# Sorted experts: weights copied to a fixed place by GpSimd, running counts on VectorE, and the last norms further behind

## The chip, the cores and the metric

The kernel runs on one core of one Trainium2 chip. The metric is the device time in microseconds of one execution, the median of several. "us" below is always microseconds, and times inside an execution count from the first instruction of the profiled one.

## The reference

Two transformer layers over x of 4 x 512 rows of 256 numbers, all in float32. Layer 0 is an attention with a delta-rule recurrence and a feed-forward block, layer 1 an attention with one key head. The last block, which the change concerns, is a mixture of eight experts. Each row picks one expert:

```python
def _L1_ffn_ref(x, Wg, W, b):
    logits = jnp.einsum('bsh,he->bse', x, Wg)
    probs = jax.nn.softmax(logits, axis=-1)
    idx = jnp.argmax(probs, axis=-1)
    onehot = jax.nn.one_hot(idx, E, dtype=x.dtype)
    combine = onehot * probs
    y = jnp.einsum('bsh,ehd->bsed', x, W) + b
    out = jnp.einsum('bsed,bse->bsd', y, combine)
    return out
...
x = _layernorm(x + _L1_ffn_ref(x, L1_ffn_Wg, L1_ffn_W, L1_ffn_b), axis=-1)
```

with E = 8 experts, W of 8 x 256 x 256 and b of 8 x 256.

## The kernel before, in words

The kernel is one program with its queues and semaphores written out by hand. Each phase is a block in which every engine has a list of instructions that it works off in order; a `wait_ge` holds all that stands behind it in the same list. The phases are the projections and the delta rule of layer 0, its attention, its feed-forward, the attention of layer 1 with its output projection (`phase_out_proj`, which also loads the experts' weights `We` and biases `be`), and `phase_moe`.

`phase_moe` sorts the 2048 rows by expert, so that a tile of 128 sorted rows needs the weights of one expert alone. Every expert's rows start at a new tile, so there are at most NTS = 16 + 7 = 23 tiles, and 23 are always worked off.

First VectorE derives from the logits a 0/1 choice `oh` for each of NT = 16 tiles of rows and 8 experts. The slot of a row is the number of rows of its expert ahead of it, plus the first slot of the expert. The rows ahead come from TensorE: a product with a triangle for the row's own tile, and 15 products with `ones` for the tiles before (L2099), each recorded as two passes. The count of each expert comes from `cs`, the sum of `oh` over the tiles (L2191), and one more product (L2102). VectorE then works out slots and the expert of each sorted tile (L2197 to L2210), GpSimd scatters the rows to `sorted_d` in DRAM with 16 indirect DMAs (L2165), and SyncE and ScalarE load them back as sorted tiles `xs`.

Then comes the loop over the 23 tiles t:

- TensorE transposes tile t+1 (`sortedT`, L2113), reads the expert's number of tile t into a register (`value_load`, L2117), multiplies with `We[:, k, e, :]` for k = 0, 1 (L2122) and adds the bias by a product of height 1 (L2123). A float32 product appears in the trace as two passes.
- ScalarE copies the transposed rows out of PSUM (L2144), then takes the root for the norm of tile t-1 (`ln.std`, L881) and writes the normalized rows of tile t-3 (`ln.apply_act`, L897).
- VectorE waits for the product of tile t, adds the residual (L2217), and does the small steps of the norm: `rstd` (L885) of tile t-1, statistics of tile t (L871), `shift` (L891) of tile t-1, mean and variance of tile t (L875). `apply_act` waits for `shift`.
- GpSimd waits for the normalized rows of tile t (`y_ok`) and scatters them to the output by an indirect DMA (L2170).

The names in the trace: `moe_sorted_rows` is xs, `moe_sorted_T` is xT, `moe_out_rows` is yo, `moe_tile_expert` the experts' numbers. Engine queues with a q behind the name (PEldq, POOLq) are the sequencer's own instructions.

## Time and profile before

| | us |
|---|---|
| median of 3 runs | 1114.26 |
| lowest, highest | 1113.63, 1125.29 |
| the profiled execution's own time | 1116.42 |
| its span, first to last instruction | 1114.7 |
| TensorE products busy | 948.9 (85%) |
| VectorE busy | 601.9 (54%) |
| ScalarE busy | 459.4 (41%) |
| GpSimd busy | 287.8 (26%) |
| mean granted clock of TensorE | 0.791 of 2.4 GHz |

The rows shown further below come from this one execution. Shares of busy time are means over all phases; what an edit in the last phase is worth has to be read from that phase, which takes from about 985 us to the end.

### The profile page before, as it was taken

Reading aid. Unit: us, or ns where it says so; the run is one execution under the profiler, and the core shown is the slowest. Engines: PE = TensorE matmul, PEld = TensorE weight load, DVE = VectorE, ACT = ScalarE, POOL = GpSimd, SP = SyncE. Lnnn points to the kernel's source line nnn. Section 1 sums busy time; section 2 is a strip of 40 time slices with the busy share of each in tenths; the row PEclk is TensorE's granted clock in tenths of the full one; section 3 lists DMA queues with packets and bytes.
Section 4 is the critical chain, followed back from the end, with each engine's and each line's share of the span. In section 5 each row is a group of like instructions: output and inputs, shape, how many; then the busy total and the mean of one; then the engine's idle time right before and its main releaser. Section 6 shows DMA issues by size and latency. Waiting matters only on the chain. (4 is left out here: it accounts for less than half of the span.)

```text
span 1114.7 us, 21534 instructions
## 1 busy us (share of the span) xinstructions
PE 948.9 (85%) x7997; PEld 617.9 (55%) x7997; DVE 601.9 (54%) x2027; ACT 459.4 (41%) x1046; POOL 287.8 (26%) x538
## 2 busy tenths in 40 slices
PE   6866715899789999979998899898999998952996
PEld 3545715777645555559874455444555554851553
DVE  1874793565467777634435344504777772820332
ACT  2553502000026666642237764631566664620232
POOL 1761112455503333310003000000333333214222
PEclk9985558555569999998879998597999999955555
DMA  5145533422200720020000000000000000405000
GB/s 116 30 84 121 192 100 104 90 61 64 57 2 1 211 58 1 1 86 1 1 21 5 1 1 1 1 1 1 2 2 1 2 1 21 171 15 169 28 30 22
DMA packets 51458, 52.28 MB, mean 47 GB/s; under 512 B 8771, under 2 KB 42905, under 8 KB 51098
## 3 DMA queue, kind: packets, MB, share of 16 engines
q1 hardware_dynamic: 41514, 39.59, 13.1%
q10 hardware_dynamic: 7488, 5.53, 2.0%
q0 software_dynamic: 2352, 5.79, 1.5%
q8 instruction: 64, 1.05, 0.4%
q14 instruction: 40, 0.32, 0.1%
HBM read 26.73 MB, written 20.88 MB: 43 GB/s over the span
## 5 line engine op out<-in xcount | busy, mean ns | idle before, releaser
L816 DVE CUSTOM_DVE_ANT_0 l_masked_scores<-psum,mask_q_rows 128x384 bf16<-128x384 f32 (+3 forms) x512 | 225.0, 488 | 76.1 <-PE psum L763 75.1
L838 ACT ACTIVATE l_probs<-psum 128x512 f32<-128x512 f32 (+1 forms) x384 | 186.3, 527 | 149.7 <-PE psum L749 149.1
L851 POOL TENSOR_SCALAR_AFFINE_SELECT l_probs<-l_probs 128x256 f32<-128x256 f32 x256 | 101.0, 406 | 379.7 <-ACT l_probs L838 379.5
L763 PE MATMUL psum<-kb_heads,q_heads 32*128 32x384 f32 (+3 forms) x512 | 108.4, 505 | 10.7 <-DVE l_neg_max_rows L805 8.7
L763 PE MATMUL psum<-l_k_heads,l_q_heads 32*128 32x384 f32 (+3 forms) x512 | 109.4, 509 | 4.6 <-DVE l_neg_max_rows L805 2.7
L749 PE MATMUL psum<-l_q_and_max,l_k_heads 32*128 32x256 f32 (+3 forms) x512 | 112.3, 472 | 0.0
L749 PE MATMUL psum<-l_q_and_max,kb_heads 32*128 32x256 f32 (+3 forms) x512 | 111.1, 467 | 0.0
L781 PE MATMUL psum<-l_probs,rows_32k 128*32 128x512 f32 (+3 forms) x1024 | 95.8, 451 | 2.9 <-POOL l_probs L851 2.9
L749 PEld LDWEIGHTS psum<-l_q_and_max,l_k_heads 32*128 32x128 f32 x512 | 58.9, 188 | 52.1 <-ACT l_probs L838 42.3
L749 PEld LDWEIGHTS psum<-l_q_and_max,kb_heads 32*128 32x128 f32 x512 | 58.3, 186 | 51.5 <-ACT l_probs L838 41.7
L641 POOL TENSOR_TENSOR v_new_and_ones<-v_and_k_rows 32x128 f32<-32x128 f32 x128 | 54.8, 445 | 51.0 <-DVE v_and_k_rows L618 47.4
L590 PE MATMUL psum<-eye_and_state,kT 32*128 32x64 f32 x1024 | 63.0, 418 | 3.3 <-issue 1.8
L763 PEld LDWEIGHTS psum<-kb_heads,q_heads 32*128 32x128 f32 x512 | 52.8, 197 | 21.2 <-DVE l_neg_max_rows L805 8.9
L763 PEld LDWEIGHTS psum<-l_k_heads,l_q_heads 32*128 32x128 f32 x512 | 53.3, 199 | 15.6 <-DVE l_neg_max_rows L816 6.3
L590 PEld LDWEIGHTS psum<-eye_and_state,kT 32*128 32x128 f32 x1024 | 57.0, 319 | 8.8 <-issue 8.6
L618 DVE TENSOR_TENSOR v_and_k_rows<-psum,own_columns 128x512 f32<-128x512 f32 x64 | 44.2, 691 | 31.4 <-PE psum L590 31.4
L838 ACT ACT_TABLE_LOAD x2 | 2.6, 1283 | 117.2 <-PEq L46 117.2
L456 PE MATMUL psum<-rows_32k,v_and_k_rows 128*32 128x128 f32 x448 | 17.2, 324 | 38.4 <-DMA rows_32k<-inverse_scratch 38.4
L597 PE MATMUL psum<-v_and_k_rows,kb_slot_rows 128*32 128x64 f32 x992 | 40.5, 314 | 6.3 <-DVE v_and_k_rows L618 6.3
L2122 PE MATMUL psum<-expert_w,moe_sorted_T 128*128 x92 | 44.4, 638 | 0.1
L816 DVE DVE_READ_ACCUMULATOR2_ANT l_neg_max_rows<- 128x1 f32 x512 | 42.4, 83 | 0.0
L1970 POOL TENSOR_TENSOR x_rows<-x_rows,last_gamma_beta 128x256 f32<-128x256 f32 x16 | 11.6, 726 | 114.3 <-PE psum L1656 114.3
(340 smaller groups left out, 1726.9 us busy)
## 6 DMA issues: line engine op xcount, KB each, us to landing
gram_scratch<-rows_32k SPq DMA_DIRECT2D x4, 1024.0 KB, 4.8
rows_32k<-v_new_and_ones SPq DMA_DIRECT2D x64, 64.0 KB, 2.6
sorted_scratch<-l1p_zeros SPq DMA_DIRECT2D x6, 494.5 KB, 8.8
x_rows<-in_L_attn_x_dram SPq DMA_DIRECT2D x16, 128.0 KB, 7.2
heads_scratch<-rows_32k SPq DMA_DIRECT2D x2, 1024.0 KB, 5.4
heads_scratch<-q_kb_T SPq DMA_DIRECT2D x2, 1024.0 KB, 5.7
inverse_scratch<-block_inv SPq DMA_DIRECT2D x2, 1024.0 KB, 4.1
q_heads<-heads_scratch SPq DMA_DIRECT2D x2, 1024.0 KB, 6.8
```

Source lines behind the costliest of these rows:

```text
L456: last = nc.tensor.matmul(ps[SLOT * j:SLOT * j + SLOT, u % 4, (2 * cc + q) * P:(2 * cc + q + 1) * P], g.VK[:, u % NP * 2 + cc, 4 * (2 * x ...
L590: last = nc.tensor.matmul(ps[:, 4 * f + j, WB * q:WB * (q + 1)], UW[r, 2 * f + q, c, :], IS[r, f, q, :, :].rearrange("p b e -> p (b e)"), ...
L597: last = nc.tensor.matmul(ps[SLOT * j:SLOT * j + SLOT, 4 * f, 2 * WB + WB * q:2 * WB + WB * (q + 1)], g.KBP[:, c, 4 * (2 * f + q) + j, :], ...
L618: nc.vector.tensor_tensor(VA[:, s % NV, f, :, :, :, :].rearrange("p j q b e -> p j q (b e)"), ps[:, 4 * f:4 * f + 4, 0:2 * WB].rearrange(" ...
L641: last = nc.gpsimd.tensor_tensor(out[:, f, :, :, :], v0, v1, ALU.add)
L749: mm = nc.tensor.matmul(ps[:, e_bank(G, u, i), o:o + w], KT(b, gq)[r, kb * P:(kb + 1) * P], QM[r, G % 2, kb * P:N], start=True, stop=True)
L763: mm = nc.tensor.matmul(ps[:, row_bank(G, u, i), o:o + w], QT(b, gq)[r, t * P:(t + 1) * P], KT(b, gq)[r, 0:w], start=True, stop=True)
L781: last = nc.tensor.matmul(ps[SLOT * j:SLOT * j + SLOT, PV_BANK, kb * P:N], va(b, kb, 4 * gq + j), PT[:, G % 2, j, o:o + w], start=(kb == 0 ...
L816: last = nc.vector.tensor_tensor_reduce(out=junk[:, ROW_AT[G, u] % 2, i, o:o + w], in0=ps[:, row_bank(G, u, i), o:o + w], in1=g.maskq[:, N ...
L838: nc.scalar.activation(PT[:, G % 2, 2 * (u % 2) + i, o:o + w], ps[:, e_bank(G, u, i), 0:w], ACT.Exp, scale=SCALE).then_inc(x_ok, 1)
L851: last = nc.gpsimd.affine_select(out=d, in_=d, pattern=[[0, 2], [1, P]], compare_op=ALU.is_ge, fill=0.0, base=0, channel_multiplier=-1)
L2122: nc.tensor.matmul(ps[:, 4 + t % 2, 0:D], xT[:, t % 2, k, :], We[:, k, bass.ds(e, 1), :].rearrange("p e n -> p (e n)"), start=(k == 0), st ...
```

## The change

1. The counting. VectorE builds running sums of `oh` over the 16 tiles in four doubling steps (`run`, each a copy of the first tiles and an addition). TensorE then needs two products with `ones`, one for the counts and one for all prefixes, in place of 15 and one.
2. The weights. GpSimd reads the expert's number into a register of its own and copies that expert's 128 x 512 weights into one of three buffers `wt` (`weights(t)`), the first three ahead of the loop and the others three tiles ahead, each written in its list before the scatter of an output tile. TensorE multiplies from `wt` and has no registers. It waits for `w_ok`.
3. The bias. `be` lies over 8 partitions, and the bias comes from a product of height 8 with a 0/1 column `own`, which now stands first in the tile's group, ahead of the wait for the transposed rows.
4. The norms. ScalarE takes the root two tiles behind (was one) and writes the normalized rows four tiles behind (was three). VectorE's `rstd` and `shift` are three tiles behind (was one).

```diff
@@ phase_moe, TensorE
             pe.wait_ge(gt, 6)
+            nc.tensor.matmul(ps[:, 0, 0:NT * E], before, oh[:, :, :].rearrange("p c e -> p (c e)"), start=True, stop=False)
+            pe.wait_ge(gt, 10)
+            pe.wait_ge(head_ok, 4)
             pe.wait_ge(or_ok, E + 1)
-            nc.tensor.matmul(ps[:, 0, 0:NT * E], before, oh[:, :, :].rearrange("p c e -> p (c e)"), start=True, stop=False)
-            for c in range(NT - 1):
-                last = nc.tensor.matmul(ps[:, 0, (c + 1) * E:NT * E], ones[:, :], bcast(oh[:, c, :], [[0, NT - 1 - c], [1, E]]), start=False, stop=(c == NT - 2))
-            last.then_inc(pre_ps, 1)
-            pe.wait_ge(gt, 7)
-            nc.tensor.matmul(ps[:, 1, 0:E], ones[:, :], cs[:, :], start=True, stop=True).then_inc(cnt_ps, 1)
-            pe.wait_ge(expert_ok, 1)
+            nc.tensor.matmul(ps[:, 1, 0:E], ones[:, :], run[:, 0, NT - 1, :], start=True, stop=True).then_inc(cnt_ps, 1)
+            nc.tensor.matmul(ps[:, 0, E:NT * E], ones[:, :], run[:, 0, 0:NT - 1, :].rearrange("p c e -> p (c e)"), start=False, stop=True).then_inc(pre_ps, 1)
+            pe.wait_ge(expert_ok, 2)
...
             def product(t):
-                e = pe.value_load(expert[0:1, t:t + 1], min_val=0, max_val=E - 1)
-                pe.wait_ge(t_sb, t + 1)
                 if t >= 2:
                     pe.wait_ge(u_ok, t - 1)
+                nc.tensor.matmul(ps[:, 4 + t % 2, 0:D], bcast(own[:, t:t + 1], [[0, P]]), be[:, :], start=True, stop=False)
+                pe.wait_ge(t_sb, t + 1)
+                pe.wait_ge(w_ok, t + 1)
                 for k in range(KD):
-                    nc.tensor.matmul(ps[:, 4 + t % 2, 0:D], xT[:, t % 2, k, :], We[:, k, bass.ds(e, 1), :].rearrange("p e n -> p (e n)"), start=(k == 0), stop=False)
-                nc.tensor.matmul(ps[:, 4 + t % 2, 0:D], ones[0:1, :], be[0:1, bass.ds(e, 1), :].rearrange("p e n -> p (e n)"), start=False, stop=True).then_inc(y_ps, 1)
+                    last = nc.tensor.matmul(ps[:, 4 + t % 2, 0:D], xT[:, t % 2, k, :], wt[:, t % 3, k, :], start=False, stop=(k == KD - 1))
+                last.then_inc(y_ps, 1)
@@ ScalarE
-            for t in range(NTS + 3):
+            for t in range(NTS + 4):
...
-                if 1 <= t <= NTS:
-                    ln.std(act, t - 1)
-                if 3 <= t:
-                    s = t - 3
+                if 2 <= t < NTS + 2:
+                    ln.std(act, t - 2)
+                if 4 <= t:
+                    s = t - 4
@@ GpSimd
+            def weights(t):
+
+                if t == 0:
+                    pool.wait_ge(expert_ok, 2)
+                    pool.wait_ge(g.we_ld, 16 * (1 + E))
+                if t >= 3:
+                    pool.wait_ge(y_ps, t - 2)
+                e = pool.value_load(expert[0:1, t:t + 1], min_val=0, max_val=E - 1)
+                nc.gpsimd.tensor_copy(wt[:, t % 3, :, :], We[:, :, bass.ds(e, 1), :].rearrange("p k e n -> p k (e n)")).then_inc(w_ok, 1)
+
+            for t in range(3):
+                weights(t)
             for t in range(NTS):
+                if t + 3 < NTS:
+                    weights(t + 3)
                 pool.wait_ge(ln.y_ok, t + 1)
                 pool.wait_ge(row_ok, t + 1)
@@ VectorE
-            step(nc.vector.tensor_reduce(cs[:, :], oh[:, :, :].rearrange("p c e -> p e c"), AX.X, ALU.add))
+            was = oh
+            for i in range(4):
+                z, now = 1 << i, run[:, (i + 1) % 2, :, :]
+                nc.vector.tensor_copy(now[:, 0:z, :], was[:, 0:z, :]).then_inc(head_ok, 1)
+                step(nc.vector.tensor_tensor(now[:, z:, :], was[:, z:, :], was[:, 0:NT - z, :], ALU.add))
+                dve.wait_ge(head_ok, i + 1)
+                was = now
...
-            nc.vector.tensor_scalar(expert[:, :], ef[:, :], float(E - 1), None, ALU.min).then_inc(expert_ok, 1)
+            step(nc.vector.tensor_scalar(ef[:, :], ef[:, :], float(E - 1), None, ALU.min))
+            nc.vector.tensor_copy(expert[:, :], ef[:, :]).then_inc(expert_ok, 1)
+            nc.vector.tensor_scalar(own[:, :], ef[0:E, :], expert_no[0:E, :], None, ALU.is_equal).then_inc(expert_ok, 1)
...
-            for t in range(NTS + 2):
+            for t in range(NTS + 3):
...
-                if 1 <= t <= NTS:
-                    ln.rstd(dve, t - 1)
+                if 3 <= t:
+                    ln.rstd(dve, t - 3)
...
-                if 1 <= t <= NTS:
-                    ln.shift(dve, t - 1)
+                if 3 <= t:
+                    ln.shift(dve, t - 3)
```

How this stands in the lists of the engines, at two places. On TensorE, in the middle of the loop, one tile before (transposes L2113 of the next tile, register steps, weight products L2122, bias L2123). Names in brackets of the kind [waits ...] are semaphores by the name under which they were first allocated in the program.

```order
L2113 MATMUL psum<-identity,moe_sorted_rows 128x128 [waits qT_sbuf,k_squared]
L2113 MATMUL psum<-identity,moe_sorted_rows 128x128
L2117 TENSOR_LOAD moe_tile_expert
L2117 ISA x2
L2122 ISA [waits qT_sbuf]
L2122 MATMUL psum<-expert_w,moe_sorted_T 128x256
L2122 ISA
L2122 MATMUL psum<-expert_w,moe_sorted_T 128x256
L2123 REGISTER_ALU
L2123 MATMUL psum<-expert_b,moe_ones 128x256
```

The same place after (L2115 the transposes, L2121 the bias, L2125 the weight products):

```order
L2115 MATMUL psum<-identity,moe_sorted_rows 128x128 [waits ffnln_mean_var_ok,kn_rows]
L2115 MATMUL psum<-identity,moe_sorted_rows 128x128
L2121 MATMUL psum<-expert_b,moe_own_expert 128x256 [waits ffnln_rstd_ok]
L2125 MATMUL psum<-moe_tile_weights,moe_sorted_T 128x256 [waits xT_in_sbuf,ffnln_mean_var_ok]
L2125 MATMUL psum<-moe_tile_weights,moe_sorted_T 128x256
```

The register instructions are gone, the bias stands ahead of the weight products, and the first of these carries two waits, for the transposed rows and for GpSimd's copy.

On GpSimd, the loop. Before, its list holds after the scatters of the rows nothing but 23 scatters of output tiles, each waiting for its normalized rows. After, this is the piece from the third copy of weights to the second scatter of an output tile:

```order
L2177 TENSOR_LOAD moe_tile_expert
L2177 ISA x2
L2178 ISA
L2178 COPY moe_tile_weights<-expert_w 128x512
L2177 TENSOR_LOAD moe_tile_expert [waits ffnln_std_ok]
L2177 ISA x2
L2178 ISA
L2178 COPY moe_tile_weights<-expert_w 128x512
L2187 DMA out_dram<-moe_out_rows,moe_row_int 2048x256 [waits ffnln_normalized,moeln_normalized]
L2177 TENSOR_LOAD moe_tile_expert [waits ffnln_std_ok]
L2177 ISA x2
L2178 ISA
L2178 COPY moe_tile_weights<-expert_w 128x512
L2187 DMA out_dram<-moe_out_rows,moe_row_int 2048x256 [waits ffnln_normalized,moeln_normalized]
```

The copies of tiles 2 and 3 stand ahead of the scatter of tile 0, the copy of tile 4 between the scatters of tiles 0 and 1, and so on up to the copy of tile 22 between those of tiles 18 and 19.

## Rows read from the trace of the kernel before

**Rows 1.** Windows: us, busy of PE, PEld, DVE, ACT, POOL, PEclk, DMA share, GB/s.

```profile
1040.00:1060.00 20.00, 20.00 (x47) 11.62 (x47) 7.20 (x36) 5.41 (x16) 5.83 (x6) 0.50 0.09 30
```

**Rows 2.** The chain that ended last: start, us, engine, what, line.

```profile
1023.08 1.08 PE psum L2113 x4
...
1038.54 1.71 PE psum L2122 x4
1040.25 1.15 PE psum L2123 x2
...
1102.45 1.16 PE psum L2123 x2
```

**Rows 3.** Timeline of one tile of the loop: start, us, engine, line, operation [idle before].

```profile
1040.18 1.22 PE L2123 MATMUL psum<-expert_b,moe_ones 1*128 x2
1041.44 0.48 DVE L2217 SCALAR_TENSOR_TENSOR moe_sorted_rows<-psum,moe_sorted_rows 128x256 f32<-128x256 f32 x1 [2.27 <-PE psum L2123]
1042.30 0.14 DVE L891 SCALAR_TENSOR_TENSOR moeln_neg_mean_rstd<-moeln_mean_var,moeln_rstd 128x1 f32<-128x1 f32 x1
1042.84 0.59 ACT L897 ACTIVATE moe_out_rows<-moe_sorted_rows,moeln_neg_mean_rstd,moeln_rstd 128x256 f32<-128x256 f32 x1
1043.65 0.50 PEld L2123 LDWEIGHTS psum<-expert_b,moe_ones 1*128 1x128 f32 x2 [0.65 <-issue]
1044.22 0.97 POOL L2170 DMA_INDIRECT out_dram<-moe_out_rows,moe_row_int  x1 [2.50 <-ACT moe_out_rows L897]
```

**Rows 4.** Timeline of the end: the last weight products and the last scatter.

```profile
1100.38 2.08 PE L2122 MATMUL psum<-expert_w,moe_sorted_T 128*128 x4
...
1108.97 0.97 POOL L2170 DMA_INDIRECT out_dram<-moe_out_rows,moe_row_int  x1 [0.30 <-issue]
```

**Rows 5.** Timeline: a product of the attention that waits for GpSimd.

```profile
937.92 0.41 POOL L851 TENSOR_SCALAR_AFFINE_SELECT l_probs<-l_probs 128x256 f32<-128x256 f32 x1 [1.04 <-ACT l_probs L838]
938.38 0.20 PEld L781 LDWEIGHTS psum<-l_probs,rows_32k 128*32 128x32 f32 x8 [1.97 <-POOL l_probs L851]
```

**Rows 6.** Timeline of the feed-forward's stage 4: two weight products, bias of height 4.

```profile
693.12 1.13 PE L1691 MATMUL psum<-stage_matrix,l_heads_out 128*128 128x256 f32 x4
...
698.31 2.08 PE L1691 MATMUL psum<-stage_matrix,l_heads_out 128*128 128x256 f32 x4
701.47 2.08 PE L1691 MATMUL psum<-stage_matrix,l_heads_out 128*128 128x256 f32 x4
...
700.32 0.50 PEld L1692 LDWEIGHTS psum<-stage_bias_rows,ffn_deviationsT 4*128 4x128 f32 x2 [0.65 <-issue]
```

**Rows 7.** Sequencers' own instructions of L2117 and L2165: ns min/median/max, first and last start.

```profile
L2117 PEldq TENSOR_LOAD <-moe_tile_expert x23: 296/302/495, 1023.1 to 1096.2; - x23
L2117 PEldq FUSED_REGOPS  x23: 151/151/165, 1023.7 to 1096.5; - x23
...
L2165 POOLq MOVE  x16: 29/29/38, 997.7 to 1005.6; - x16
```

**Rows 8.** Groups of GpSimd by form: busy us, mean ns of one, idle before.

```profile
L851 POOL TENSOR_SCALAR_AFFINE_SELECT l_probs<-l_probs 128x256 f32<-128x256 f32 x256 | 101.0, 406 | 379.7 <-ACT l_probs L838 379.5
L196 POOL TENSOR_TENSOR rope_t<-rows_32k,rope_sin 128x512 f32<-128x512 f32 x14 | 19.4, 1405 | 6.8 <-DVE k_sumsq L237 6.7
L532 POOL COPY eye_and_state<-slot_eye_and_minus_one 128x128 f32<-128x128 f32 x2 | 1.2, 612 | 4.1 <-DMA own_columns<-in_chain_dram 4.1
L1582 POOL MEMSET l0p_bias_slots<- 128x512 f32 x1 | 0.5, 524 | 3.8 <-POOLq L46 3.8
```

**Rows 9.** Timeline of the counting, and the last of 16 scatters of rows.

```profile
987.73 0.38 DVE L2191 TENSOR_REDUCE moe_tile_choices<-moe_choice 128x8 f32<-128x128 f32 x1
988.34 6.41 PE L2099 MATMUL psum<-moe_choice,moe_ones 128*128 128x120 f32 x30
994.53 0.55 PEld L2102 LDWEIGHTS psum<-moe_tile_choices,moe_ones 128*128 128x128 f32 x2
995.26 0.29 DVE L2197 TENSOR_TENSOR moe_over_limit<-psum,routing_consts 128x128 f32<-128x128 f32 x1 [6.55 <-PE psum L2102]
1017.86 0.97 POOL L2165 DMA_INDIRECT sorted_scratch<-rows_and_choice,moe_slot_int  x1 [0.30 <-issue]
```

More of the change, by code:

```diff
@@ L925, in _ @@
             sp.dma_start(g.route[:, :], g.route_d).then_inc(g.route_ld, 16)
-            sp.dma_start(g.be[:, :, :], bass.AP(tensor=g.d["L1_ffn_b"].tensor, offset=g.d["L1_ffn_b"].offset, ap=[[E * D, 1], [1, E * D]])).then_inc(g.we_ld, 16)
+            sp.dma_start(g.be[:, :], g.d["L1_ffn_b"]).then_inc(g.we_ld, 16)
             for e in range(E):
@@ L2052 @@
 ZW = NTS * XW // NZERO
-ROUTE = list(itertools.accumulate((0, NT, E * E, NTS, NT, P)))
+ROUTE = list(itertools.accumulate((0, NT, E * E, NTS, NT, P, 1)))
 def phase_moe(nc, g):
@@ L2064, in phase_moe @@
         We, be, XR, rt = g.We, g.be, g.XR, g.route
-        lim, below, tile_no, row_no, before = (rt[:, ROUTE[i]:ROUTE[i + 1]] for i in range(5))
+        lim, below, tile_no, row_no, before, expert_no = (rt[:, ROUTE[i]:ROUTE[i + 1]] for i in range(6))
         lg, pr, oh = sb("logits", [P, NT, E]), sb("exps", [P, NT, E]), sb("choice", [P, NT, E])
         mxl, sm, first = sb("max", [P, NT]), sb("sum", [P, NT]), sb("first_rank", [P, NT])
-        cs, cm, tl, tm, st, en = (sb("tile_choices", [P, E]), sb("over_limit", [P, E, NT]), sb("tiles", [P, E]), sb("tiles_below", [P, E, E]), sb("first_tile", [P, E]), sb("end_tile", [P, E]))
+        run = sb("choices_so_far", [P, 2, NT, E])
+        cm, tl, tm, st, en = (sb("over_limit", [P, E, NT]), sb("tiles", [P, E]), sb("tiles_below", [P, E, E]), sb("first_tile", [P, E]), sb("end_tile", [P, E]))
         pf, pos, slot = sb("slots", [P, NT, E]), sb("slot", [P, NT]), sb("slot_int", [P, NT], I32)
         te, expert = sb("tiles_past", [P, NTS, E]), sb("tile_expert", [P, NTS], I32)
-        ef = sb("tile_expert_f", [P, NTS])
+        ef, own = sb("tile_expert_f", [P, NTS]), sb("own_expert", [E, NTS])
         order, ones = sb("order", [P, E]), sb("ones", [P, P])
@@ L2074, in phase_moe @@
         xT, yo = sb("sorted_T", [P, 2, KD, P]), sb("out_rows", [P, 4, D])
+        wt, w_ok = sb("tile_weights", [P, 3, KD, D]), sem("tile_weights_ok")
+        head_ok = sem("first_tiles_copied")
         or_ok, gt, ex_ok, id_ok, pre_ps, cnt_ps, slot_ok, expert_ok = (sem("order_ok"), sem("gate_steps"), sem("exps_ok"), sem("row_numbers"), sem("before_psum"), sem("count_psum"),
@@ L2160, in _ @@
             pool.wait_ge(g.zero_st, 16 * NZERO)
-            pool.wait_ge(gt, 9)
+            pool.wait_ge(gt, 12)
             pool.wait_ge(id_ok, 1)
@@ L2298, in program @@
                 phase_attention(nc, g, "l1", OT, lambda b, gq: g.QT1[:, gq, b, :], lambda b, gq: g.KT1[:, b, :], False, HD, lambda b, kb, h: g.VA1[:, 4 * b + kb, :])
-            g.XR, g.route, g.be = (ctx.enter_context(nc.sbuf_tensor(n, s, F32, side="right")) for n, s in (("rows_and_choice", [P, NT, XW]), ("routing_consts", [P, ROUTE[-1]]), ("expert_b", [1, E, D])))
+            g.XR, g.route, g.be = (ctx.enter_context(nc.sbuf_tensor(n, s, F32, side="right")) for n, s in (("rows_and_choice", [P, NT, XW]), ("routing_consts", [P, ROUTE[-1]]), ("expert_b", [E, D])))
             phase_out_proj(nc, g, OT)
@@ L2322, in consts @@
         "route": np.concatenate([np.tile(P * np.arange(NT), (P, 1)), np.tile(np.tril(np.ones((E, E)), -1).reshape(1, -1), (P, 1)), np.tile(np.arange(NTS), (P, 1)),
[L2323 removed]
+                                 2 * B * N - (N * (q // R) + R * np.arange(NT)[None, :] + q % R), q < k, q], 1).astype(np.float32),
         "ones": np.ones((1, N), np.float32),
```

1 line of the change is left out of this document (removed).

## The prediction

> **What bounds the kernel now.** I read the windows first. In the stage of the sorted experts TensorE is busy for 20.00 of 20 us, at a granted clock of 0.50, which is 1.2 GHz of its two levels [rows 1]. The chain that ended last agrees: from the first sorted tile (1023.08) to the end of the last product (1103.61) it runs on TensorE alone, one tile every 3.47 us (the 80.5 us over 23 tiles come to 3.50), of which the four passes of the two weight products take 1.71 and the bias product 1.15 [rows 2]. The timeline of one tile shows the others waiting: after the bias product ends (1040.18 + 1.22 = 1041.40), VectorE adds the residual at 1041.44, the shift of the norm is done at 1042.44, ScalarE writes the normalized rows until 1043.43, and GpSimd issues the scatter at 1044.22 [rows 3]. GpSimd is idle some 2.5 us of each 3.47. So an edit saves here only what it takes off TensorE's own row of work, and it costs nothing until some other engine, or a loop through several, needs more than 3.47 us a tile.
>
> **Part 1, the counting of choices.** Before, one vector reduction (987.73) and thirty short passes on TensorE (6.41 us) stand between the choice and the counts, and VectorE waits for them until 995.26 [rows 9]. After, VectorE makes running sums in four steps, each a small copy and an addition of at most 128x120. An operation of that size takes 0.29 (the 995.26 row), and I add 0.13 for the copy and the hand-over: 4 x 0.42 = 1.7, from 987.73 to 989.4. The count product then needs what it needs now, 994.53 to 995.26 = 0.73 [rows 9], so VectorE goes on at 990.15 and no longer at 995.26: **-5.1 us**. Bounds 4.5 to 5.5. The sum and reciprocal of the softmax, two operations of under 0.3, fit ahead of 990.15, and the product for the prefixes (two passes, 0.43 by the thirty in 6.41) is done before its reader, four vector operations later. The extra three small operations at the end of the list stand behind the slots, on which GpSimd's scatter depends, so they delay nothing. All later work starts 5.1 earlier.
>
> **Part 2, TensorE without registers.** It removes a register load (0.30) and a register step (0.15) a tile [rows 7], but these are the sequencer's. Do they show on TensorE? A tile has six passes of 0.43 (1.71 / 4) and two transposes of half that length: 2.99. The tile takes 3.47, so 0.48 are lost, and the trace puts them at two places where the next weight load stood still for 0.65 "issue", at the bias product and behind it [rows 3]. The feed-forward stage has the same pair of products, weights over 128 rows and a bias over 4, with no register at all: same 0.65, and 3.16 a tile for six passes, that is 0.30 for each change between few rows and 128 [rows 6]. So the loss belongs to the change of height, not to the registers, and the change keeps both changes (transposes to an 8-row bias, bias to products). I cost the removal at nothing, and the new order at +0.11 a tile, as two full changes of 0.30 take the place of 0.48 (over the first three tiles +0.35). The Trainium skill, "TensorE: Matmul & The Clock Gate", part 3, What overlaps and what doesn't, says that a weight load overlaps a running product only where the row groups differ. The rows here show the reverse, loads hidden between products of equal height and exposed where the height changes, and the measurement decides; by the page's rule the bias's load would be free, and the sum would be 0.3 a tile lower wherever TensorE is the bound.
>
> **Part 3, GpSimd's copies, and what they are queued behind.** Each weights(t) is a register load, two register steps and a copy of 128x512. A register load on a sequencer took 0.30 [rows 7]. GpSimd's sequencer runs far ahead of its engine: the last MOVE of the 16 scatters stands at 1005.6 [rows 7], the last scatter itself at 1017.86 [rows 9]. So I hide the 0.5 us of registers behind the scatter queued before. For the copy the nearest rows are a fill of 128x512 (0.52, no input), a product of two inputs 128x512 (1.41), and one input 128x256 (0.406) [rows 8]; the last is likest in kind, and twice it less one start-up gives 0.75, which I take, with 0.52 and 1.41 as the ends. (Two 128x128 copies took 0.61 on average [rows 8], more per element; if that held the copy would be over 2 us. They read a repeated view at the start of the scan, and I hold it unlikely.) The Trainium skill, "GPSIMD Engine Reference", section 3.1, gives 769 ns for 512 elements in the best loop; by this estimate a tile would be 0.02 longer than by mine.
>
> The price of the copy matters less than its place. GpSimd's list is W3, D0, W4, D1, ... (W weights, D scatter of the output). D(s) waits for the normalized rows of tile s. The norms are moved back: VectorE computes the shift of tile s behind the residual of tile s+3, which waits for product(s+3). W(s+4) stands behind D(s) in the list, and product(s+4) now waits for W(s+4). So **product(s+4) can't start until product(s+3) has gone round the whole loop**: VectorE, ScalarE, scatter, copy. The three buffers of weights don't help, since the copy ahead is held by the scatter's wait. Before, no such loop existed, as nothing TensorE reads came from GpSimd. Round the loop, at 1.2 GHz:
> - residual to shift, 1041.44 to 1042.44: 1.00 [rows 3]
> - hand-over 0.04 (1041.40 to 1041.44), normalized rows 0.59 [rows 3]
> - to the scatter's start, 1043.43 to 1044.22: 0.79; the scatter 0.97 [rows 3]
> - from scatter to copy: two scatters in a row stand 0.30 apart [rows 4], and the least is nothing; I take 0.15. The copy 0.75
> - GpSimd to TensorE 0.05 (938.33 to 938.38) [rows 5]; four passes from a standstill 2.08 [rows 4]; hand-over 0.04
>
> Sum 6.46 a tile against 3.47. Transposes, bias product (before the wait) and the copy of the transposed rows fit beside it. Tiles 4 to 22 are bound so, 19 times: 19 x 2.99 = **+56.8 us**. Tiles 0 to 3 aren't: W0 to W2 run after the last scatter of rows, while TensorE still waits 4 us for the landing, and W3 needs only product(0).
>
> **Part 4, the tail.** Before, from the end of the last product (1102.45 + 1.16 = 1103.61 in the chain [rows 2]) to the end of the last scatter (1108.97 + 0.97 [rows 4]) are 6.33. After: four scatters remain behind the last product: 0.04 + 1.00 + 0.04 + 0.59 + 0.79 + 3 x 1.27 + 0.97 = 7.24, so **+0.9**.
>
> **Sum**: -5.1 + 0.35 + 56.8 + 0.9 = +52.9. The profiled execution took 1116.42 (span 1114.7), 2.2 above the median of 1114.26; the difference goes on the median: 1167.
>
> **Rivals.**
> - *TensorE stays the bound*: the loop that I read isn't closed, because scatter and copy overlap somewhere. Then a tile takes 3.58: -5.1 + 23 x 0.11 + 0.9, time 1112.6. For it speaks only the plan of three buffers; against it the order of the list. 0.04.
> - *TensorE stays the bound and the registers were its stalls* (the side of faster): 3.47 falls to 2.99, 23 x 0.48 = 11.0 less, 1114.3 - 5.1 - 11.0 + 0.9 = 1099. It decides if the 8-row load is hidden. Against it [rows 6]. 0.02.
> - *The clock rises* to 2.4 GHz in the loop: four passes then take 1.13 in place of 2.08 [rows 6], a tile 5.51, and +38.8 in place of +56.8: 1149. At 20 of 20 us busy the clock stood at 0.50 [rows 1], and now TensorE pauses 3 us a tile. [...] 0.04.
> - *The loop is closed and dearer*: registers not hidden (+0.5), copy 1.41 (+0.66), gap 0.30 (+0.15): 7.77 a tile, 1192. *Cheaper*: copy 0.52, no gap: 6.08, 1160. Both belong to my forecast, 0.90.
>
> **How the numbers follow.** Forecast 1167; the range takes both ends of the loop and some for the parts read to 0.1: 1158 to 1192. A change within 1% (11 us) is what this measurement can't tell from none. Slower by more: loop 0.90 + clock 0.04 = 0.94; within: 0.04; faster: 0.02.
>
> **What would show it.** GpSimd's copy right behind each scatter and TensorE idle some 3 us ahead of the first weight product from tile 4 on, released by GpSimd; products of tiles 1 to 3 at the old pace; 6 to 7 us a tile; the clock at 0.50; the counts on VectorE at 990 and not 995. A pace near 3.5 would refute the loop; a pace of 8 or more would mean that the registers or the copy are dearer than any row here.

## The result, and the profile after

The changed kernel takes 1166.54 us (median of 4 runs, 1156.07 to 1175.24) against 1116.13 of the kernel before beside it (1113.63 to 1125.29): ratio 1.041, 95% interval 1.036 to 1.046. The ratio leaves out the slow run of 1175.24, without which the median is 1165.16. The forecast was 1167, the range 1158 to 1192. The profiled execution took 1165.16, its span 1163.4 (before 1116.42 and 1114.7).

The windows of the changed kernel over the stretch of [rows 1] (columns as there):

```profile
1040.00:1060.00 20.00, 10.86 (x24) 6.42 (x24) 3.60 (x18) 3.16 (x9) 5.72 (x7) 0.50 0.05 16
```

TensorE is busy for 10.86 us of 20 where it was busy for 20.00, no other engine is above 6.42, and the clock still stands at 0.50. Nothing is the bound by its own work, which is how a loop through several engines looks in windows. The timeline of one tile shows it; the numbers in brackets are idle time and what ended it:

```profile
1041.95 2.05 PE L2125 MATMUL psum<-moe_tile_weights,moe_sorted_T 128*128 128x256 f32 x4 [2.66 <-POOL moe_tile_weights L2178]
1044.04 0.48 DVE L2242 SCALAR_TENSOR_TENSOR moe_sorted_rows<-psum,moe_sorted_rows 128x256 f32<-128x256 f32 x1 [5.08 <-PE psum L2125]
...
1044.90 0.14 DVE L891 SCALAR_TENSOR_TENSOR moeln_neg_mean_rstd<-moeln_mean_var,moeln_rstd 128x1 f32<-128x1 f32 x1
1045.08 0.60 ACT L897 ACTIVATE moe_out_rows<-moe_sorted_rows,moeln_neg_mean_rstd,moeln_rstd 128x256 f32<-128x256 f32 x1 [5.23 <-DVE moeln_neg_mean_rstd L891]
1046.48 0.98 POOL L2187 DMA_INDIRECT out_dram<-moe_out_rows,moe_row_int  x1 [4.67 <-ACT moe_out_rows L897]
1047.44 0.64 POOL L2178 COPY moe_tile_weights<-expert_w 128x512 f32 x1
...
1048.23 2.05 PE L2125 MATMUL psum<-moe_tile_weights,moe_sorted_T 128*128 128x256 f32 x4 [2.65 <-POOL moe_tile_weights L2178]
```

Read from top to bottom it is one chain: products, residual, shift (done at 1045.04), normalized rows (done at 1045.68), 0.80 later the scatter, and the copy of the weights right behind the scatter, for which the next products wait. From products to products are 6.28 here. The chain that ended last repeats the same circle, 1130.46 to 1136.79 = 6.33:

```profile
1130.46 2.06 PE psum L2125 x4
...
1133.09 0.39 DVE moeln_stats L871
...
1133.64 0.61 ACT moe_out_rows L897
...
1136.02 0.64 POOL moe_tile_weights L2178
...
1136.79 2.06 PE psum L2125 x4
```

In [rows 2] the same chain lay on TensorE alone. The waits between 1045 and 1140 (engine, what waited, for whom: us in total, times, longest), and the row of L2178 with those who waited for it:

```profile
ACT moe_out_rows L897 <- DVE moeln_neg_mean_rstd L891: 84.3, 16, 5.3
DVE moe_sorted_rows L2242 <- PE psum L2125: 76.8, 15, 5.1
POOL out_dram L2187 <- ACT moe_out_rows L897: 70.8, 15, 4.7
...
PE psum L2125 <- POOL moe_tile_weights L2178: 40.5, 15, 2.7
```

```profile
L2178 POOL COPY moe_tile_weights<-expert_w x23: 617/626/639, 1012.3 to 1148.7; 128x512 f32 x23
...
  PE psum L2125: 51.8, 19
```

Every engine waits for the one ahead of it in the circle, and TensorE waits for the copy 19 times: tiles 4 to 22. The first of these waits ends at 1035.67. The tiles before it still run at TensorE's pace (the 0.65 in the first line is the stall at a change of height, as in [rows 3]; the profile puts it down to ScalarE's copy, which ran at 1028.29 for 0.37 and so was long done):

```profile
1029.32 1.36 PEld L2125 LDWEIGHTS psum<-moe_tile_weights,moe_sorted_T 128*128 128x128 f32 x4 [0.65 <-ACT moe_sorted_T L2147]
1029.33 2.08 PE L2125 MATMUL psum<-moe_tile_weights,moe_sorted_T 128*128 128x256 f32 x4
...
1035.67 0.76 PE L2125 MATMUL psum<-moe_tile_weights,moe_sorted_T 128*128 128x256 f32 x1 [2.70 <-POOL moe_tile_weights L2178]
```

The counting, beside [rows 9]:

```profile
986.50 0.17 DVE L2211 COPY moe_choices_so_far<-moe_choice 128x8 f32<-128x8 f32 x1
986.58 0.28 DVE L2212 TENSOR_TENSOR moe_choices_so_far<-moe_choice 128x120 f32<-128x120 f32 x1
...
988.04 0.59 PE L2103 MATMUL psum<-moe_choices_so_far,moe_ones 128*128 128x8 f32 x2 [0.73 <-DVE moe_choices_so_far L2212]
...
988.73 0.29 DVE L2220 TENSOR_TENSOR moe_over_limit<-psum,routing_consts 128x128 f32<-128x128 f32 x1
```

And the tail, beside [rows 4]: four scatters in a row, 1.28 from one to the next.

```profile
1154.04 0.97 POOL L2187 DMA_INDIRECT out_dram<-moe_out_rows,moe_row_int  x1 [4.74 <-ACT moe_out_rows L897]
...
1157.87 0.98 POOL L2187 DMA_INDIRECT out_dram<-moe_out_rows,moe_row_int  x1 [0.30 <-issue]
```

From both traces, measured between the same instructions (the copy of the logits opens the phase; a tile's mark is the start of VectorE's residual):

| stretch | before | after | difference |
|---|---|---|---|
| logits to counts on VectorE | 9.47 | 4.17 | -5.30 |
| counts to the first scatter of rows | 3.30 | 3.30 | 0.00 |
| first scatter to the residual of tile 3 | 39.40 | 39.41 | 0.01 |
| residual of tile 3 to that of tile 22 | 65.68 | 120.09 | +54.41 |
| residual of tile 22 to the end of the last scatter | 6.30 | 7.32 | +1.02 |
| sum | 124.15 | 174.29 | +50.14 |

The medians differ by 50.4, the profiled executions by 48.7; the latter also contain 1.2 us by which the phase happened to begin earlier in the run after.

### The profile page after: what moved, and what is told of

It reads as the page before. It is cut to its first block and busy times, and to the rows that moved or that the text cites. A ratio compares the mean times of both kernels' runs of the same rounds, so it can differ in the third digit from the quotient of the medians.

```text
span 1163.4 us, 21466 instructions
## 1 busy us (share of the span) xinstructions
PE 938.7 (81%) x7969; PEld 608.2 (52%) x7969; DVE 603.3 (52%) x2036; ACT 460.1 (40%) x1046; POOL 301.1 (26%) x561
## 5 line engine op out<-in xcount | busy, mean ns | idle before, releaser
L763 PE MATMUL psum<-kb_heads,q_heads 32*128 32x384 f32 (+3 forms) x512 | 109.3, 509 | 10.7 <-DVE l_neg_max_rows L805 8.7
L2125 PE MATMUL psum<-moe_tile_weights,moe_sorted_T 128*128 128x256 f32 x92 | 47.1, 668 | 51.8 <-POOL moe_tile_weights L2178 51.8
L2242 DVE SCALAR_TENSOR_TENSOR moe_sorted_rows<-psum,moe_sorted_rows 128x256 f32<-128x256 f32 x23 | 11.1, 484 | 108.8 <-PE psum L2125 108.8
L2125 PEld LDWEIGHTS psum<-moe_tile_weights,moe_sorted_T 128*128 128x128 f32 x92 | 27.0, 324 | 71.6 <-issue 64.9
L897 ACT ACTIVATE moe_out_rows<-moe_sorted_rows,moeln_neg_mean_rstd,moeln_rstd 128x256 f32<-128x256 f32 x23 | 13.6, 598 | 103.6 <-DVE moeln_neg_mean_rstd L891 103.6
L2187 POOL DMA_INDIRECT out_dram<-moe_out_rows,moe_row_int x23 | 22.5, 977 | 102.5 <-ACT moe_out_rows L897 101.6
```

The costliest lines, as they stand in the source:

```text
L763: mm = nc.tensor.matmul(ps[:, row_bank(G, u, i), o:o + w], QT(b, gq)[r, t * P:(t + 1) * P], KT(b, gq)[r, 0:w], start=True, stop=True)
L897: self.nc.scalar.activation(out, x, ACT.Identity, scale=self.rs[:, s, :], bias=self.nm[:, s, :]).then_inc(self.y_ok, 1)
L2125: last = nc.tensor.matmul(ps[:, 4 + t % 2, 0:D], xT[:, t % 2, k, :], wt[:, t % 3, k, :], start=False, stop=(k == KD - 1))
L2187: nc.gpsimd.indirect_dma_start(out=g.out.rearrange("b n d -> (b n) d"), out_offset=bass.IndirectOffsetOnAxis(ap=row[:, t:t + 1], axis=0), ...
```

## The experiments

Ratios are to the kernel before on the same chip, with 95% intervals; "interval" without more is the time from one tile's residual to the next, in the trace. Where no ratio is given the kernel ran once, and what counts is its trace. A "tall" bias product reads 128 rows and not 1 or 8: the biases stand in every partition, and the weight is one in a single row and zero in the others, so that the result is the same.

### Opening the loop: e1_four_ahead

The changed kernel with a fourth buffer for the weights, and each copy one place further ahead in GpSimd's list, so that the copy for tile s+4 stands ahead of the scatter of tile s:

```diff
-        wt, w_ok = sb("tile_weights", [P, 3, KD, D]), sem("tile_weights_ok")
+        wt, w_ok = sb("tile_weights", [P, 4, KD, D]), sem("tile_weights_ok")
...
-                if t >= 3:
-                    pool.wait_ge(y_ps, t - 2)
+                if t >= 4:
+                    pool.wait_ge(y_ps, t - 3)
...
-                if t + 3 < NTS:
-                    weights(t + 3)
+                if t + 4 < NTS:
+                    weights(t + 4)
```

> The changed kernel with a fourth buffer of weights, and weights(t+4) ahead of the scatter of tile t in GpSimd's list (was t+3). Nothing else differs. Loop theory: the round VectorE, ScalarE, scatter, copy, products (6.33 us in the changed kernel) now spans two tiles, 3.17 a tile, less than TensorE's own 3.58 (its pace in tiles 0 to 3), so the pace falls to 3.58 and the time to about 1114 (before 1116, less 5.3 for the counting, plus 2.5 for the pace, plus 0.9 for the tail). Rival, the hand-over itself is slow (reading weights that GpSimd has just written, or GpSimd's two jobs in turn): the order in the list doesn't matter, the pace stays at 6.3 and the time near 1166.

Measured: 1116.64, ratio 0.999 (0.995 to 1.003). The interval is 3.58 from the first tile on (the last, with no transposes ahead of it, is 3.15). Its timeline has the same operations at the same prices (copy 0.64, scatter 0.98, products 2.07), only nobody waits for the copy:

```profile
1051.20 0.64 POOL L2178 COPY moe_tile_weights<-expert_w 128x512 f32 x1
...
1052.84 2.07 PE L2125 MATMUL psum<-moe_tile_weights,moe_sorted_T 128*128 128x256 f32 x4
1053.81 0.98 POOL L2187 DMA_INDIRECT out_dram<-moe_out_rows,moe_row_int  x1 [1.98 <-ACT moe_out_rows L897]
```

GpSimd does as much work as in the slow kernel and all 50 us are gone. The loss is the closed loop, not the copies.

### Opening it at the other end: e2_norms_as_before

The changed kernel, three buffers, with the norms at the lag that they had before:

```diff
-                if 4 <= t:
-                    s = t - 4
+                if 3 <= t:
+                    s = t - 3
...
-                if 3 <= t:
-                    ln.shift(dve, t - 3)
+                if 1 <= t <= NTS:
+                    ln.shift(dve, t - 1)
```

(and `std` and `rstd` likewise).

> The changed kernel with the norms where they were before: root one tile behind, normalized rows three, VectorE's small steps one. Weights still by GpSimd, three buffers, same list. Loop theory: the rows that a scatter waits for hang on the product two tiles back, not one; a round is 2.0 (end of product to normalized rows, as before) + 1.76 + 0.63 + 0.11 + 2.05 = 6.6 over two tiles, 3.3 a tile, so TensorE's 3.58 binds: about 1113. Rival, the copies by GpSimd cost the time whatever the norms do: near 1166, pace 6.3.

Measured: 1114.65, ratio 0.995 (0.992 to 0.999), interval 3.58, and TensorE is full again:

```profile
1040.00:1060.00 20.00, 20.00 (x47) 11.94 (x45) 7.03 (x35) 5.21 (x15) 9.60 (x12) 0.50 0.08 26
```

ScalarE's write of tile s now stands behind the root of tile s+2, so scatter s needs the products of s+2, and the copy behind it serves those of s+4: the circle has two tiles, 7.16 at 3.58 each, and is shorter than that. Lag and copy ahead are each harmless; together they make the loop.

### The counting alone: e3_count_only

The kernel before with the running counts and nothing else of the change:

```diff
-            for c in range(NT - 1):
-                last = nc.tensor.matmul(ps[:, 0, (c + 1) * E:NT * E], ones[:, :], bcast(oh[:, c, :], [[0, NT - 1 - c], [1, E]]), start=False, stop=(c == NT - 2))
...
+            nc.tensor.matmul(ps[:, 1, 0:E], ones[:, :], run[:, 0, NT - 1, :], start=True, stop=True).then_inc(cnt_ps, 1)
+            nc.tensor.matmul(ps[:, 0, E:NT * E], ones[:, :], run[:, 0, 0:NT - 1, :].rearrange("p c e -> p (c e)"), start=False, stop=True).then_inc(pre_ps, 1)
```

> The kernel before with the new counting alone (running sums on VectorE, two products with ones). VectorE goes on to the counts some 5.2 us earlier after the choice, the loop keeps its 3.47 a tile: 1111, which is inside what times can tell, so the trace decides. Rival: the scatters don't start earlier since they wait for something else (zeroed scratch, GpSimd): the gap from choice to first scatter stays at 10.8 us.

Measured: 1115.16, ratio 0.999 (0.995 to 1.003). The times can't tell this from no change. The trace can: logits (992.88) to counts (997.04) are 4.16, as after, against 9.47 before; the first scatter of rows follows 3.30 later, as before and after, so the rival is out; the interval stays 3.47. A saving of 5.3 is shown by the trace and lies at the edge of what the runs of this kernel resolve.

### Doubling the suspect: e4_copy_twice

The changed kernel with a second copy of the same weights into a buffer that nobody reads, ahead of the real one:

```diff
+                nc.gpsimd.tensor_copy(twin[:, t % 3, :, :], We[:, :, bass.ds(e, 1), :].rearrange("p k e n -> p k (e n)"))
                 nc.gpsimd.tensor_copy(wt[:, t % 3, :, :], We[:, :, bass.ds(e, 1), :].rearrange("p k e n -> p k (e n)")).then_inc(w_ok, 1)
```

> The changed kernel with each copy of weights preceded by a second one into a buffer that nobody reads. Loop theory: the copy stands on the loop, so 19 tiles take 0.63 more each, pace 6.96, and the time rises by 12.0. Rival, GpSimd's copies are hidden and the wait is for another link: pace stays at 6.3.

Measured in one run: 1180.81; intervals 3.58 three times, then 6.82 to 7.14 for a few tiles and 6.87 to 6.88 for the rest, that is 0.55 more than 6.33, where 0.63 was expected. From tile 3 to tile 22 it takes 10.7 us longer than the changed kernel; 12.0 was expected. Its timeline:

```profile
1066.54 0.98 POOL L2189 DMA_INDIRECT out_dram<-moe_out_rows,moe_row_int  x1 [4.73 <-ACT moe_out_rows L897]
1067.51 0.62 POOL L2179 COPY moe_tile_weights_twin<-expert_w 128x512 f32 x1
1068.06 0.62 POOL L2180 COPY moe_tile_weights<-expert_w 128x512 f32 x1
1068.83 1.62 PE L2126 MATMUL psum<-moe_tile_weights,moe_sorted_T 128*128 128x256 f32 x3 [3.26 <-POOL moe_tile_weights L2180]
```

Every copy behind the scatter is paid in full on the circle, and starts 0.55 after the one ahead, a little before that one's recorded end (0.62). In e1, with the loop open, the copies cost nothing.

### Are registers the stalls? e5_tall_bias_registers

The kernel before, registers and all, with the bias product at the height of the others:

```diff
-                nc.tensor.matmul(ps[:, 4 + t % 2, 0:D], ones[0:1, :], be[0:1, bass.ds(e, 1), :].rearrange("p e n -> p (e n)"), start=False, stop=True).then_inc(y_ps, 1)
+                nc.tensor.matmul(ps[:, 4 + t % 2, 0:D], bcast(g.idf[:, 0:1], [[0, P]]), be[:, bass.ds(e, 1), :].rearrange("p e n -> p (e n)"), start=False, stop=True).then_inc(y_ps, 1)
```

> The kernel before, registers and all, with the bias product of height 128 in place of 1: the biases lie on all partitions, and the weights of the product are a column of the identity, so only row 0 counts. Same passes, same columns. Height theory: the two stalls of 0.65 at the weight loads are due to the change of height, so they go and a tile takes 2.99 in place of 3.47; 1116 - 11 = 1105, or less if the granted clock rises, as the array is now used at full height all the time. Rival, the stalls are the registers': the pace stays at 3.47 and the time at 1116.

Measured: 1087.13, ratio 0.971 (0.966 to 0.976), far more than the stalls were worth. In its timeline the weight loads of the bias and of the transposes have no idle time ahead of them, with the register step where it was; and the products are half as long:

```profile
1041.33 1.13 PE L2122 MATMUL psum<-expert_w,moe_sorted_T 128*128 x4
1042.08 0.41 PEld L2123 LDWEIGHTS psum<-expert_b,identity 128*128 128x128 f32 x2
1042.29 0.59 PE L2123 MATMUL psum<-expert_b,identity 128*128 x2
1042.51 0.36 PEld L2113 LDWEIGHTS psum<-identity,moe_sorted_rows 128*128 128x128 f32 x2
```

The windows give the reason, the granted clock (third column from the end):

```profile
1020.00:1030.00 10.00, 4.24 (x13) 3.24 (x14) 0.35 (x2) 2.03 (x3) 0.98 (x2) 0.50 0.68 207
1040.00:1050.00 10.00, 8.97 (x43) 7.04 (x42) 5.76 (x29) 5.21 (x15) 5.20 (x6) 1.00 0.13 46
```

TensorE goes from 1.2 to 2.4 GHz within the first tiles, where before it stayed at 1.2 through 20.00 of 20 us busy [rows 1]. Tiles then alternate at 1.68 and 2.29, 1.99 on average, since TensorE now waits for ScalarE's copy of the transposed rows.

### Both together: e6_tall_bias_four_norms and e7_tall_bias_three_norms

e6 is the changed kernel with four buffers, the norms' lag of before and the tall bias product (the eight bias rows repeated over the partitions; the tile's expert is compared with the partition's number, so one row of 128 counts). e7 is e6 with three buffers again.

```diff
-            sp.dma_start(g.be[:, :], g.d["L1_ffn_b"]).then_inc(g.we_ld, 16)
+            sp.dma_start(g.be[:, :], bass.AP(tensor=g.d["L1_ffn_b"].tensor, offset=g.d["L1_ffn_b"].offset, ap=[[0, P // E], [D, E], [1, D]])).then_inc(g.we_ld, 16)
...
-            nc.vector.tensor_scalar(own[:, :], ef[0:E, :], expert_no[0:E, :], None, ALU.is_equal).then_inc(expert_ok, 1)
+            nc.vector.tensor_scalar(own[:, :], ef[:, :], expert_no, None, ALU.is_equal).then_inc(expert_ok, 1)
```

> The changed kernel with four buffers of weights (weights four tiles ahead), the norms where they were before, and the bias product of height 128 (the biases repeated over the partitions, the 0/1 column zero beyond row 7). The loop through GpSimd spans three tiles, 6.6 / 3 = 2.2, so it doesn't bind. Height theory: 2.99 a tile, 1116 - 5.3 - 11 = 1100; if the clock rises to 2.4 GHz, VectorE or the loop binds next at 2.2 or so and the time goes to 1080. Rival (the height isn't what stalls): 3.58 a tile, 1113.

> As the one with four buffers, but with three (weights three tiles ahead, as in the changed kernel). The loop through GpSimd spans two tiles: end of product to normalized rows 2.03, to the scatter 0.80, scatter 0.98, copy 0.63, to TensorE 0.11, products 2.05 = 6.60, 3.30 a tile. Loop theory: it binds, at 3.30 and not at TensorE's own 2.99, some 6 us more than with four buffers. Rival, a scatter or copy may run ahead of its place in the list: 2.99 as with four.

Measured: e6 1077.21, ratio 0.964 (0.959 to 0.970), at 2.4 GHz, mean interval 1.91. e7, in one run, 1099.79: tiles 0 to 3 at 1.51 to 1.52, then 4.20, 1.77 and 4.84, and from tile 6 on mostly 2.18 and 3.49 in turn, 2.84 on average. Its expectation took the clock to stay at 1.2 GHz; it rose. With that put right, the expected circle of 6.60 over two tiles loses 2.08 - 1.13 = 0.95 and is 5.65, or 2.83 a tile: as measured from tile 6 on. Over the three tiles of e6 the same circle would be 1.88 a tile, near the 1.91. In e7, before tile 6, the clock fell back to 0.50 for some 3 us, after TensorE had stood idle for 2.15 us:

```profile
1039.79 2.04 PE L2125 MATMUL psum<-moe_tile_weights,moe_sorted_T 128*128 128x256 f32 x4 [2.15 <-POOL moe_tile_weights L2178]
```

```profile
1040.00:1043.00 3.00, 3.00 (x9) 2.35 (x10) 1.13 (x6) 0.00 (x0) 1.41 (x2) 0.50 0.06 19
```

An idle time of 2.45 a little earlier (1031.67 to 1034.12) had left it at 2.4 GHz. So the norms' lag that was harmless at 3.58 a tile in e2 closes a loop over two tiles as soon as TensorE is faster, and the fourth buffer, worth nothing there, is worth 0.9 a tile here.

### Where the 0.11 comes from: e8_bias_last

e1 with the bias product (height 8) last in the tile, as before the change, and still no register on TensorE:

```diff
-                nc.tensor.matmul(ps[:, 4 + t % 2, 0:D], bcast(own[:, t:t + 1], [[0, P]]), be[:, :], start=True, stop=False)
...
+                last = nc.tensor.matmul(ps[:, 4 + t % 2, 0:D], bcast(own[:, t:t + 1], [[0, P]]), be[:, :], start=False, stop=True)
```

> The changed kernel with four buffers of weights (TensorE bound, 3.58 a tile) and the bias product, still of height 8, last in its tile as in the kernel before, and still no registers. If the place of the bias made the 0.11 by which 3.58 exceeds the 3.47 of before, this one has 3.47 exactly, and the registers cost nothing at all. Rival, the registers did cost something and height 8 costs more than height 1: another pace, 3.58 or below 3.47.

Measured in one run: 1120.01. The first intervals are 3.48, 3.47, 3.47, 3.47, those of the kernel before with its registers (3.47) and not 3.58. Then they alternate at 3.47 and 4.00, 3.73 on average, which the expectation missed: with four buffers the circle goes over two tiles, and the bias product now lies in it. From the start of the weight products to the residual are 3.23 (1062.32 to 1065.55 below) where they were 2.09, so the circle is 6.33 + 1.14 = 7.47, or 3.73 a tile. This working was made afterwards. The timeline has the wait in every second tile:

```profile
1061.56 0.62 POOL L2178 COPY moe_tile_weights<-expert_w 128x512 f32 x1
1062.32 2.04 PE L2124 MATMUL psum<-moe_tile_weights,moe_sorted_T 128*128 128x256 f32 x4 [0.19 <-POOL moe_tile_weights L2178]
...
1065.55 0.48 DVE L2242 SCALAR_TENSOR_TENSOR moe_sorted_rows<-psum,moe_sorted_rows 128x256 f32<-128x256 f32 x1 [2.80 <-PE psum L2125]
```

### Registers at full clock: e9_registers_late

e5 with the running counts and the changed kernel's lag of the norms: no copies on GpSimd at all.

> The kernel before (registers on TensorE, nothing on GpSimd but scatters) with the new counting, the bias product of height 128 and the norms as far behind as in the change. Without copies by GpSimd the late norms close no loop. In the run with the tall bias and the old norms a tile took 1.68 and 2.29 in turn at 2.4 GHz, the longer ones waiting for ScalarE's copy behind a root. If that wait is due to the near norms, it goes: 1.68 a tile, about 6 us less than that run, 5 more by the counting: 1087 - 11 = 1076. Rival, another link holds ScalarE (the statistics themselves): 2.0 a tile, 1082.

Measured: 1079.09, ratio 0.964 (0.960 to 0.968). The long lag costs nothing where TensorE doesn't wait for GpSimd, and gains a little (1.84 for the 1.99 of e5). Undisturbed tiles take 1.51 to 1.52, like those of e7 without registers: a register load a tile is free at 2.4 GHz too. The expected 1.68 for every tile was wrong: intervals alternate at 1.52 and 2.18, 1.84 on average from tile 4 on, and the waits of the trace (1035 to 1060) name ScalarE's write of normalized rows (L897) waiting for VectorE's shift, with the copy of the transposed rows queued behind it:

```profile
ACT moe_out_rows L897 <- DVE moeln_neg_mean_rstd L891: 11.1, 14, 1.1
```

### Copies further ahead: e10_copies_six_late

The changed kernel with the tall bias, six buffers and copies six tiles ahead, late norms kept:

```diff
+        wt, w_ok = sb("tile_weights", [P, 6, KD, D]), sem("tile_weights_ok")
...
+                if t + 6 < NTS:
+                    weights(t + 6)
```

> The changed kernel with the tall bias and six buffers of weights, weights six tiles ahead; norms as in the change. The loop now spans four tiles, 5.3 / 4 = 1.3, and doesn't bind. GpSimd has a scatter and a copy per tile; where it ran without waits these took 1.77 together, more than TensorE's 1.51. So GpSimd is the bound: 1.77 a tile, 1074 to 1079, and no better than the version with registers, whose tile is 1.68. Rival: copies cost nothing, 1.51 a tile and about 4 us less than the version with registers.

Measured: 1077.29, ratio 0.963 (0.958 to 0.968); intervals of 1.76 to 1.77 from tile 7 on (one is 1.82), as expected the pace of GpSimd, on which a scatter and a copy come to that:

```profile
1048.89 0.62 POOL L2178 COPY moe_tile_weights<-expert_w 128x512 f32 x1
1049.04 0.49 DVE L891 SCALAR_TENSOR_TENSOR moeln_neg_mean_rstd<-moeln_mean_var,moeln_rstd 128x1 f32<-128x1 f32 x1
...
1049.67 0.98 POOL L2187 DMA_INDIRECT out_dram<-moe_out_rows,moe_row_int  x1 [0.17 <-issue]
```

Nobody waits for a copy here (the trace from 1045 to 1060 names none), so the weights are not what hands GpSimd's pace on. VectorE's shift is the likely link: where it starts under a copy it takes 0.38 to 0.55 in place of 0.14 and ends 0.02 to 0.03 behind the copy, 15 tiles in a row; ScalarE's write and the copy of the transposed rows come behind it. No run moves the copy away from the shift, so this link is read, not tested. Only with TensorE this fast do the copies cost anything by themselves.

### How tall? e11_bias_64_rows

The kernel before with the bias product over 64 rows.

```diff
-                nc.tensor.matmul(ps[:, 4 + t % 2, 0:D], bcast(g.idf[:, 0:1], [[0, P]]), be[:, bass.ds(e, 1), :].rearrange("p e n -> p (e n)"), start=False, stop=True).then_inc(y_ps, 1)
+                nc.tensor.matmul(ps[:, 4 + t % 2, 0:D], bcast(g.idf[0:64, 0:1], [[0, P]]), be[0:64, bass.ds(e, 1), :].rearrange("p e n -> p (e n)"), start=False, stop=True).then_inc(y_ps, 1)
```

(the minus line is that of e5)

> The kernel before with a bias product of height 64 in place of 1. It separates what raised the granted clock in the tall version. If the clock rose because the stalls at the change of height went away, this one (height still changes, stalls of 0.65 stay) keeps 1.2 GHz and 3.47 a tile. If it rose because more rows of the array are in use, height 64 may be enough: 2.4 GHz and about 2 us a tile with the stalls still there, of 0.33.

Measured in one run: 1099.76. Windows (columns as in [rows 1]):

```profile
1040.00:1050.00 10.00, 10.00 (x24) 5.65 (x23) 3.17 (x16) 3.13 (x9) 2.92 (x3) 0.50 0.07 26
1050.00:1060.00 10.00, 9.81 (x32) 5.55 (x31) 4.14 (x23) 4.17 (x12) 2.92 (x3) 0.74 0.09 31
1060.00:1070.00 10.00, 9.63 (x41) 5.59 (x39) 5.90 (x30) 4.73 (x14) 4.87 (x5) 1.00 0.14 48
```

Six tiles run at 3.47 with stalls of 0.65, exactly as before; then the clock rises with the stalls still there, and the intervals go to 1.86 and 2.30. Stall and clock are two things: 64 rows make the same stall as one, and the clock rises without its going.

### The last wait: e12_writes_five_late

e9 with the write of the normalized rows one tile later in ScalarE's list:

```diff
-                if 4 <= t:
-                    s = t - 4
+                if 5 <= t:
+                    s = t - 5
```

> The kernel of e9 (registers on TensorE, bias product at height 128, running counts, late norms) with one more step of lag: ScalarE writes the normalized rows of tile s in its turn s+5, not s+4. In e9 the intervals alternate 1.52 and 2.18 (mean 1.84), and the long ones fall where ScalarE's copy of the transposed rows stands behind a write of normalized rows that waits for VectorE's shift. If that place is the cause, the wait goes and every tile takes 1.52, the 1.51 to 1.52 of the undisturbed pairs, and GpSimd (0.97 + 0.30 = 1.27 a scatter) still keeps up: 18 x 0.32 = 5.8 less in the loop, one more scatter of 1.27 behind the last product, so about 1074.5 and 4.5 under e9. Rival: the long intervals have another cause (VectorE's own list, or the clock), then the alternation stays at a mean of 1.84 and the time comes out 1.3 over e9, about 1080.

Measured: 1073.5, ratio 0.961 (0.958 to 0.965), median of 6 runs. Intervals are 1.51 to 1.53 in the first half (after a first one of 2.39), 1.56 to 1.57 in the second (one is 1.74), 1.55 on average between tiles 3 and 22, and TensorE is full again, now at 2.4 GHz:

```profile
1035.00:1055.00 20.00, 20.00 (x106) 17.11 (x104) 14.89 (x75) 13.51 (x39) 12.51 (x13) 1.00 0.20 68
```

It is the fastest kernel of the study, 43 us under the one before and some 93 under the changed one; its lead over e6, e9 and e10 is within their intervals.

## Why the prediction was right

**The mechanism** was that of part 3, and e1 and e2 show it from both ends: open either side of the circle and 3.58 a tile comes back. The wait falls where it was forecast, 19 times, tiles 4 to 22.

**The size of the loop**: 6.46 forecast, 6.32 measured on average, and the 19 intervals cost 54.4, not 56.8. By terms, in the tile shown (6.28; most take 6.33, with 0.10 for 0.04 between shift and rows): the copy takes 0.63 (forecast 0.75); it starts right behind the scatter (0 for 0.15); from the copy's end to the first product are 0.15 (0.05); residual to shift 1.00, rows 0.60, to the scatter 0.80, scatter 0.96, products with their hand-over 2.09: all within 0.03. So 0.27 too much for the copy and its gap stand against 0.10 too little for the way to TensorE. The copy's price came from the nearest row of one input at half the size, [rows 8], and was 0.12 too dear; leaving the two small copies aside, which would have made it over 2 us, came out right, but why they took 0.61 no run shows.

**Registers on GpSimd** were hidden, as forecast: the register load (median 289 ns) starts 0.59 behind the normalized rows and ends 0.08 into the scatter (1046.27 to 1046.55), the steps behind it are done at 1046.87, and the scatter runs until 1047.46. From the rows to the scatter are 0.80, which were 0.79 before without it [rows 3].

**Registers on TensorE**: costed at nothing for their removal, and e8 shows it at 1.2 GHz (3.47 with and without), e9 and e7 at 2.4 GHz (1.51 to 1.52 with and without). The rival by which the registers were the stalls is refuted by e5, in which the stalls go and the registers stay. That the new place of the bias product costs 0.11 is right to the digit (3.58; back to 3.47 in e8). The 0.3 a tile at the end of part 2 counts one side alone: a rule by which loads are hidden only where the heights differ would also leave the loads between equal heights exposed, and in [rows 3]'s tile those start while the product ahead still runs (1042.24 under a product that ends at 1042.44).

**The first tiles**: +0.35 forecast, 0.01 measured. The term is mis-sized because it counted only the three intervals (3.47 to 3.58, which are there). The first tile itself came 0.31 earlier. Of this, 0.18 lies between its transposes and its residual (4.46 before, 4.28 after): with the bias product ahead, TensorE does it while ScalarE copies the transposed rows (1017.12 to 1017.92), which the forecast didn't look at. The other 0.13 lie ahead of the transposes, which began sooner behind the first scatter (24.39 for 24.52) as the sorted rows arrived sooner; nothing in the edit speaks for that.

**The counting**: -5.30 for -5.1. The four steps took 1.5 us from 986.50 to 988.02, where 1.7 was forecast; copy and addition of a step overlap. e3 shows the same alone.

**The tail**: +1.02 for +0.9.

**The clock** stayed at 0.50 although TensorE paused 2.65 us a tile, so the rival at 1149 did not occur. Its ground in the prediction was thinner than it looked: e5 and e11 show that a small edit of one product moves the clock, and [rows 1] alone could not have told that.

**Luck**: 1166.54 for 1167 is closer than the sum was. The difference of the medians was forecast 2.5 us too large (52.9 for 50.4), and the kernel before came out 1.9 us slower beside the changed one (1116.13) than in the runs that the forecast went by (1114.26); the two nearly cancel. The changed kernel's own runs spread over 19 us.

## What to carry to other kernels

Before making one engine copy ahead for another, write down that engine's list and look at what each copy is queued behind: if it stands behind a wait for the consumer's own results, count over how many tiles the circle goes and compare its length with so many tiles at the present pace. Depth of buffers, place in the list and lag of the late steps are one budget, and it must be counted anew whenever the bound engine becomes faster (e2 against e7). When the bound engine is full, compare its passes with each other before removing instructions from its sequencer: here the register was free, and a product over one row that looked cheap cost some 30 us, mostly by the clock (e5: 1.99 a tile at 2.4 GHz for 3.47 at 1.2 GHz).
